# Moving a rounding, its remainders and the order of the last finishes in a wavelet, convolution and median kernel

## The reference, cut to what matters

```python
cA, cH, cV, cD = dwt2(x)                        # Haar bands, 16 x 16 each
proc  = lambda c: batchnorm_relu(conv1x1(c, conv_w))   # statistics over all images
rimg0 = idwt2(proc(cA), proc(cH), proc(cV), proc(cD))
rimg1 = three-level Haar transform and back     # is x again
y = conv3x3(concat([rimg0, rimg1]), convW_w) + convW_b
x = batchnorm_relu(y)                           # statistics over all images
m = median_3x3(x)                               # zero padding
out = x + conv1x1(m, W) + b
```

## Time and profile before

| | us |
|---|---|
| median of three executions | 408.54 |
| lowest, highest | 407.53, 408.69 |
| the profiled execution | 409.56 |
| its span | 407.2 |

### The profile page before, as it was taken

One profiled execution on the slowest core, in us unless ns is written; L12 is line 12 of the kernel. 1 busy time (PEld: TensorE's weight loads), 2 busy tenths in 40 slices (PEclk: granted clock), 3 DMA queues, 4 the chain that ended last, 5 costly groups with the idle time before them and its releaser, 6 DMA issues.

```text
span 407.2 us, 3844 instructions
## 1 busy us (share of the span) xinstructions
PE 391.0 (96%) x1202; PEld 223.2 (55%) x1202; DVE 372.8 (92%) x528; ACT 168.5 (41%) x364; POOL 216.8 (53%) x208
## 2 busy tenths in 40 slices
PE   7889999999999999999999999999999999988994
PEld 2325568877544445555554545454656788833441
DVE  2899975999949999999999999999999999898995
ACT  2466764423244533333434334242424222473861
POOL 3999769234724547557374847557343530042341
PEclk9999999999999999999999999999999999999998
DMA  7980010010101010110101010110101000004554
GB/s 284 417 355 2 2 52 2 0 52 2 52 0 52 1 52 2 52 47 5 53 0 52 1 53 1 52 43 11 52 0 52 2 0 1 2 0 179 233 222 190
DMA packets 7794, 26.70 MB, mean 66 GB/s; under 512 B 992, under 2 KB 1248, under 8 KB 7776
## 3 DMA queue, kind: packets, MB, share of 16 engines
q1 hardware_dynamic: 7776, 26.48, 17.1%
HBM read 18.09 MB, written 8.39 MB: 65 GB/s over the span
## 4 chain that ended last, share of the span: by engine, by line
PE 77%; DVE 8%; POOL 7%; issue 3%; DMA 2%; ACT 2%; SPq 0%; POOLq 0%; DVEq 0%
PE conv_ps L423 57%; PE conv_ps L438 10%; PE conv_ps L540 4%; PE one_ps L405 3%; PE one_ps L516 2%; POOL y L244 2%; POOL y L245 2%; DMA z<-x 2%; PE conv_ps L543 1%; DVE y L998 1%; POOL y L382 1%; ACT z L706 1%; DVE one_ps L865 1%; DVE one_ps L922 0%; DVE sorted_cols L918 0%
## 5 line engine op out<-in xcount | busy, mean ns | idle before, releaser
L423 PE MATMUL conv_ps<-ru,wt 128*128 128x512 f32 (+1 forms) x360 | 131.1, 500 | 0.0
L423 PEld LDWEIGHTS conv_ps<-ru,wt 128*128 128x128 f32 x360 | 68.1, 190 | 49.5 <-issue 45.7
L423 PE MATMUL conv_ps<-xu,wt 128*128 128x496 f32 (+3 forms) x240 | 87.5, 501 | 0.0
L655 ACT ACTIVATE y<-conv_ps,sgn 128x512 f32<-128x512 f32 (+1 forms) x40 | 25.5, 637 | 130.9 <-PE conv_ps L423 130.9
L423 PEld LDWEIGHTS conv_ps<-xu,wt 128*128 128x128 f32 x240 | 45.4, 190 | 31.9 <-issue 28.6
L251 POOL TENSOR_TENSOR ru<-z 128x512 f32<-128x512 f32 x14 | 18.1, 1294 | 59.1 <-DVE one_ps L907 59.1
L423 PE MATMUL conv_ps<-ru,v 128*128 128x496 f32 (+3 forms) x120 | 43.8, 501 | 0.6 <-POOL ru L252 0.5
L344 POOL TENSOR_TENSOR ru<-eo 128x512 f32<-128x512 f32 x16 | 17.0, 1061 | 45.3 <-DVE one_ps L865 45.1
L540 PE MATMUL conv_ps<-z,w 128*128 128x512 f32 x64 | 31.3, 623 | 5.7 <-DVE y L998 3.4
L405 PE MATMUL one_ps<-y,w 128*128 128x512 f32 x64 | 30.4, 605 | 5.6 <-DVE z L745 3.2
L610 ACT ACTIVATE z<-z,bn 128x256 f32<-128x256 f32 x64 | 33.0, 591 | 1.9 <-DVE bn L810 1.9
(11 more groups left out here) (141 smaller groups left out, 756.2 us busy)
## 6 DMA issues: line engine op xcount, KB each, us to landing
z<-x SPq DMA_DIRECT2D x16, 512.0 KB, 11.0
raw_place<-x SPq DMA_DIRECT2D x15, 512.0 KB, 3.2
out<-y SPq DMA_DIRECT2D x15, 512.0 KB, 2.6
wt<-w_t SPq DMA_DIRECT2D x2, 576.0 KB, 10.5
ru<-x SPq DMA_DIRECT2D x1, 512.0 KB, 14.0
out<-y SPq DMA_DIRECT2D x2, 256.0 KB, 2.0
w<-w_t SPq DMA_DIRECT2D x2, 64.0 KB, 7.8
vec<-vectors SPq DMA_DIRECT2D x1, 3.0 KB, 9.9
```

The lines of the kernel that those rows point to most:

```text
L423: return nc.tensor.matmul(bank(u, b)[:, (r0 - row) * BW:(r1 - row) * BW], taps(half, kx, ky), plane[:, (r0 + dy) * BW:(r1 + dy) * BW], sta ...
L655: S.activation(at(slot(n), row * W + b, [[2, cols]]), src, ACT.Identity, scale=sgn[:, :], accum_out=y_sum[:, part:part + 1]).then_inc(y_ke ...
```

## The change

SUMMED goes from images 3, 6, 9 and 12 to images 2, 5, 8 and 11, so OWN is 0, 1, 3, 4, 6, 7, 9, 10, 12, 13, 14, 15. The second batch norm is put behind step 9. Eight finishes (images 0, 1, 3, 4, 6, 7, 9, 10) stand behind steps 16, 20, 24 and so on to 44, where nine (0, 1, 2, 4, 5, 7, 8, 10, 11) stood behind steps 16, 19, 22 and so on to 40. The finishes of 12, 13, 14 and the two halves of 15 follow the last median; before, those of 13, 14 and 15 did.

At the start of stage 2, POOL makes ru03 of images 0 and 1 directly behind xu03 and the wait for x_edges; the two remainders of the taps follow, and the remainder x_lo of image 2 is made in the loop, behind ru12 of image 2. ACT rounds image 2 not ahead of the first square root but behind the norms of image 2, directly ahead of keep_y of unit 0.

```diff
-    SUMMED = (3, 6, 9, 12)
+    SUMMED = (2, 5, 8, 11)
-    BN3_AT, FINISH_AT = 7, (16, 19, 22, 25, 28, 31, 34, 37, 40)
+    BN3_AT, FINISH_AT = 9, (16, 20, 24, 28, 32, 36, 40, 44)
...
             for n in range(2):
                 make_xu03(n)
-            make_lo(2)
+            pool.wait_ge(x_edges_made, 2)
+            for n in range(2):
+                make_ru03(n)
             for b in range(2):
                 pool.wait_ge(hi_taps_made, b + 1)
                 G.tensor_tensor(tap_part(taps_lo, b), whole_taps(b), tap_part(fl(taps_hi), b), ALU.subtract).then_inc(lo_taps_made, 1)
-            pool.wait_ge(x_edges_made, 2)
-            for n in range(2):
-                make_ru03(n)
...
                 make_ru12(G, n).then_inc(ru12_made, 1)
-                if n in SPLIT[1:]:
+                if n in SPLIT:
                     make_lo(n)
...
-            wait_xu12(act, SPLIT[0])
-            round_x(SPLIT[0])
             act.wait_ge(var1_ready, 1)
...
+            round_x(SPLIT[0])
             for u in range(len(UNITS)):
```

## The result

| | before | after |
|---|---|---|
| median of four executions each, us | 408.6 | 405.4 (404.9 to 405.87) |
| profiled execution / its span, us | 409.56 / 407.2 | 405.87 / 403.6 |
| ratio, 95% interval | | 0.992 (0.9903 to 0.9936) |

The account below looks back on a forecast made before the run. PE was taken to lead until about 355 us, then PE and DVE in turn; +0.2 - 1.1 - 3.5 - 0.2 + 0.5 = -4.1 us gave 404.4 us against the 408.54 median, range 402.8 to 406.9.

Parts of the forecast that it names:

- What leads where: Whole kernel: PE leads from 41.8 to about 355 us; behind that no engine leads for long.
- The reader who booked the 2.8 us: First batch norm: the port rule alone books the whole 2.5 to 3 us as gain, some 401.6 us.
- Part 1: The start, moved rounding and remainders: PE gains at most 0.3 us, rounding makes it wait; +0.2 us, bounds -0.2 and +0.9.
- Parts 2 and 3: Tail: first finish -1.1 us by later batch norm 3; from there to last median -3.5 us, fewer finishes, less idling.
- Part 4: Behind the last median: 5.9 us instead of 6.07 at full clock, -0.2 us; stores +0.5 us.
- (a): Rival, end of tail: the clock falls again before mix 15 or 14, another 1.7 us, 406.1 us; 12%.
- (b): Rival, tail: idle time is only moved and DVE's 3.1 us return, 407.0 us; 9%.
- (c): Rival, tail: total DVE work is the same and the clock falls as well, 408.2 us, no difference; 6%.
- (d): Rival, tail: PE's holes before mixes 9 and 12 lower the clock from mix 12 on, 411.3 us, slower; 4%.
- (e): Rival, start and tail: rounding's cover holds and no map meets line 865, -5.8 us, 402.8 us; 7%.

Follow-up runs that it names:

- fit_and_round: place_fit with the rounding of image 2 behind keep_p of unit 2 instead of ahead of keep_y of unit 0; 403.23 us, 0.9872 of the kernel before.
- places_only: Kernel before with the eight finish places every fourth step, old summed images, batch norm 3 behind step 7; 410.33 us, ratio 1.0021.
- summed_only: Kernel before with images 2, 5, 8, 11 summed, nine finishes at the old steps, batch norm 3 behind step 7; 411.13 us, ratio 1.0054.
- place_fit: Changed kernel with batch norm 3 behind step 10 and nine finishes behind steps 16, 18, 25, 28, 32, 33, 40, 42, 46; 403.49 us, ratio 0.9885.
- after_bn_early: Changed kernel with batch norm 3 back behind step 7; 406.28 us, 0.9931 of the kernel before.
- start_only: Changed kernel with the tail's old numbers, so only the start of the change; 409.15 us, 1.0005 of the kernel before.
- bn_late_only: Kernel before with only batch norm 3 moved behind step 9 instead of 7; 407.81 us, ratio 0.997.
- before_again: Kernel before, unchanged, run again for a second trace; 409.13 us, ratio 1.0007.

## Why the prediction was right

**What leads where** was read rightly. Up to 355 us everything hangs on PE: of the freed 2.8 us of the first batch norm only 0.5 us reached PE, since line 516 keeps it busy, and the rounding took those back. The reader who booked the 2.8 us by the Trainium skill's rule on shared ports (SBUF — State Buffer, SBUF: two separate sides) would have been right about the delay and wrong about its worth.

**Part 1** was mis-sized by 0.2 us net, and it is partly luck that it was no more. The gain that reaches PE was put at no more than 0.3 us and was 0.50. The wait for ACT came, 0.23 us long, but ACT's own queue hung on PE's earlier products, which came 0.33 us sooner where I had granted 0.1, so that the squares ended at 65.89 - 0.69 = 65.20 in the time of the kernel before, 0.25 us or more earlier than the 65.45 to 65.55 worked out. Taking the wait away brought 0.5 us (fit_and_round). How the 0.50 us divide between the earlier norms and POOL's earlier ru03 no run shows.

**Parts 2 and 3** hit: -1.22 and -3.6 for -1.1 and -3.5. Here the method is worth more than the numbers. Both lists, of places and of summed images, act only together: the extra product of a summed image has to fall into a hole of PE, and each finish has to come when its product is ready and before PE needs the bank. Alone they cost 0.8 and 1.1 us against the first trace of the kernel before, 2.0 and 2.3 against the second, 1.5 and 2.3 timed. What I had put into the sum as separate savings (one finish fewer, less idle time) are two sides of one schedule.

**Part 4** is the step that failed in size. The sum took the profiled execution's 3.55 us for image 15 as what the kernel before always pays, and so 6.07 us behind the last median. The same kernel paid 4.93 us in its second trace. The changed kernel has no such hole and takes 6.02 us in both of its traces. The sum then took 1.0 us off for the profiled execution's distance from the median and kept the whole -4.1, as if the median execution paid for the clock in full. With 4.93 us in place of 6.07 the term would have been +1.0 instead of -0.2 and the sum -2.9, where 3.2 and 3.0 us were timed. The load stage can hardly be that execution's extra 1.0 us: it ended early there (41.82, where the 14 traces have 42.2 on average). The timed changes of the whole table say the same: they fit the second trace of the kernel before, not the first. How much an average timed execution of the kernel before pays for the clock is still not measured, since only the traced ones show it.

**The rivals.** (a), a clock that falls again, did not come in either trace of the changed kernel; all sixteen matmuls of the last four images took 0.43 us from start to start. (b) and (c) fell with DVE's idle time, 0.5 us as laid out. (d) fell with them: PE's longest hole in this tail was 0.78 us in the records. What (d) describes happened in places_only, behind a hole of 2.32 us before mix 3. (e) did not hold: line 863 met the map and took 1.25 us.

## What to carry to other kernels

Where two engines hand buffers to each other in a hand-written order, lay out the tail instruction by instruction with start-to-start times from the trace; sums of savings do not add there, while a layout gave the end of the changed kernel to 0.3 us (of places_only only to 0.8, with its last median missed by 1.5), and it found places worth another 1.65 us in the trace (1.9 between the medians). Compare two traces from an instant behind the loads, not from zero. Before a forecast from one trace is moved onto the median, ask where in the trace its distance from the median lies, and whether the change removes it. Price a clock fall at a hole as a range, as two executions of one kernel paid 0.4 and 1.6 us for it. A rounding, a copy or a map costs nothing only if it also misses the queue that releases the leading engine and the instructions that it would hold up.

## What the runs showed of the hardware

In these traces a DVE instruction with both operands in SBUF (the core's on-chip memory) was held by POOL's map, which works on SBUF data, where it started 0.17 us or more behind the map: line 863 took 1.25 us and ended 0.24 us behind the map, where it takes 0.39 alone, and line 864 took 1.34 (summed_only) and 1.31 (places_only) against 0.46. Where it started 0.18 us ahead of the map (place_fit), it took 0.39 us and the map 1.27 instead of 1.20. Where both are shown as starting within 0.09 us (after_bn_early), line 863 took 0.40 us and the map 1.40. That line 865 is held was known from the kernel before; new to me was how much the worth of an edit (1.3 us of an earlier finish, 0.5 left) can hang on 0.1 us between two starts.

PE holes of 2.28 us (two traces of the kernel before, start_only, bn_late_only), 2.32 us (places_only) and 4.98 us (summed_only) were followed by a granted clock of 0.50 (1.2 GHz) in part or all of the next image; holes of 1.61 and 1.76 us were not. How much it takes differs between executions: 3.55 and 2.40 us for image 15's four matmuls in the kernel before, 2.84 in start_only, 3.65 in bn_late_only, 1.96 at the full level. In before_again and start_only the image began at a granted clock of 1.00 and the clock fell to 0.50 while it ran.
